# A fused cross-attention and feed-forward kernel: one weight factor split later, and one store of sums cut in three

## The chip, the cores and the metric

The kernel runs on one core of a Trainium2 chip. The metric is the device time of one execution in microseconds (us), the median of the runs. The core has a matrix engine (TensorE, PE in the profile, with its weight loads under PEld), three elementwise engines (VectorE or DVE, ScalarE or ACT, GpSimd or POOL) and SyncE (SP), whose queue issues nearly all of this kernel's transfers (DMAs). The engines run their own instruction streams in order and meet at semaphores.

## The reference, cut to what matters

```python
x = x + tanh(g_xattn) * attention(layernorm(x), ctx, ctx, Wq, Wk, Wv, Wo)   # 32 heads, 8 key/value heads
xt = layernorm(x).reshape(-1, 1024)                                        # 16 * 128 = 2048 tokens
x = x + tanh(g_ffn) * ((silu(xt @ W_gate.T) * (xt @ W_up.T)) @ W_down.T)   # hidden width 2752
```

Everything is float32. Each product is made from three matmuls of operands that are split in a high part, rounded to the matrix engine's format (`_h`), and the low rest (`_l`): high by high, high by low, low by high.

## The kernel before, in words

**Stages.** First the attention, in NG = 4 groups of four sequences (`body`). Then the feed-forward part in NS = 2 passes `s` over the tokens. Each pass has a gate/up phase and a down phase. Both use a scheme with seven products of half size instead of eight (Strassen-Winograd), so sums and differences of blocks are made ahead of the products.

**Gate/up.** For each of 21 blocks of hidden units (`quad`; the very first is `first_quad`) seven products are made. Product j takes the weight factor `w_h[j]`, `w_l[j]` and the token operand `xop_h[j]`, `xop_l[j]`. ACT makes the high part of a factor (`weight_hi`), DVE the low one (`weight_lo`). Factors 1, 2, 4 and 5 are sums of weight blocks that POOL makes into `fs`. In pass 0 the token operands are made around and inside the first quad: PE transposes a piece (`first_tokens(n)`, n = 0 to 27, four pieces for each operand) into one of two PSUM banks, ACT copies its high part (`first_tokens_hi`), DVE subtracts for its low part (`first_tokens_lo`). With only two banks, `first_tokens(n)` on PE waits until piece n-2 has its low part (`xp_lo`, n-1). In product 0 pieces 8 to 11 are transposed, one behind each of its four steps of the contraction, and so on. The fifth factor (j = 4) is copied by ACT once `xp_done` is 8 and `ts_ready` is 16, where 16 means that POOL has finished the last of the sums `t4`. This is needed because its place in memory was taken by other data until then. In the kernel before, this copy stands just ahead of `first_quad` on both ACT and DVE. On DVE there stand behind it five low parts (pieces 8 to 12), the halves of the attention's last addition (`add_half`), and its statistics, each between two low parts.

**Down.** The hidden values of two blocks are a pair; there are PAIRS_B = 11 pairs. POOL makes five sums of a pair in `hsum` (five matrices of 256 KB), and they are stored to DRAM in `hs`. A down phase has 77 steps, seven products (`m`) of eleven pairs (`q`). Step n has q = n mod 11. For each step SP loads two matrices of 256 KB into one of RAWS = 4 buffers `raw` (`load_down`: one from `hs`, one from `ws` or `wd`), ACT copies the high part (`bh`, one of three buffers, `down_hi`), DVE subtracts the low part (`bl`, `down_lo`), and PE runs four groups of three matmuls (in some steps of pass 0 with transposes for the next pass among them). `load_down(n)` waits until step n-4 has its low part. `down_hi(n)` waits until PE is through with step n-3. At a change of product (n = 11, 22, ...) DVE also adds the finished sums into `xo` (`add_down`).

**The place of the store.** SP issues in the order of the program. At the end of `gate_up` stand `load_down(7)`, `load_xo(C12)` (1 MB), `load_down(8)` and the store of the last pair's five sums (1280 KB in one DMA), which waits for POOL. Then `down` goes on with `load_down(9)`, `load_down(10)`, `load_down(11)`, `load_xo(C22)` (1 MB), `load_down(12)`. `load_down(11)` is the first step of the second product and waits until all eleven stores of sums of the pass have landed. POOL's `pair_sums` for pass 1 also waits for them, because its `ts` lies on `hsum`.

Of the kernel before, what the change touches and what calls it, by code (L numbers as in the profile page):

```python
# [99 lines left out]
def gated_cross_attention_ffn(nc, x, ctx_t, wc, wr, wf, wm, wd, g_xattn, g_ffn, x1d, hs, ws, out):  # L100

    with ExitStack() as ctx:
# [114 lines left out]
        def sem(name):  # L217
            return ctx.enter_context(nc.semaphore(name))
# [69 lines left out]
        h_ready = sem("h_ready")  # L288
        ha_out, hb_out, hs_out = sem("ha_out"), sem("hb_out"), sem("hs_out")
        hs_ready = sem("hs_ready")  # L290
        hb_zero = sem("hb_zero")
        dw_in = sem("dw_in")
        ws_ready, ws_out = sem("ws_ready"), sem("ws_out")
# [47 lines left out]
        def pairs(s, c, i):  # L341
            return i + (PAIRS_B * s + c // 2)
# [29 lines left out]
        def _(sp):  # L372
# [137 lines left out]
            def store_sums(s, c, i):  # L510
                sp.wait_ge(hs_ready, summed(s, c, i, H_SUMS))
                sp.sem_inc(passed, 1)
                sp.dma_start(of_pair(hs[s], i + c // 2)[0:H_SUMS].rearrange("m p n -> p m n"), hsum[:, :, :]).then_inc(hs_out, 16)

            def load_dw(q, i):
                if q == 0:
                    sp.wait_ge(xp_done, 28)
                else:
                    sp.wait_ge(ws_out, i * 32 + 32 * q)
                sp.sem_inc(passed, 1)  # L520
                src = wd[2 * q:2 * q + 2] if isinstance(i, int) else wd[bass.ds(i * 2 + 2 * q, 2)]
                sp.dma_start(dw[:, :, :], src.rearrange("t p n -> p t n")).then_inc(dw_in, 16)
# [9 lines left out]
            def load_down(s, n):  # L532
                m, q = n // PAIRS_B, n % PAIRS_B
                k = n % RAWS
                hx, wx, _ = DOWN[m]
                if n >= RAWS:
                    sp.wait_ge(b_lo, step(s, n - RAWS))
                elif n < 2:
                    sp.wait_ge(ws_out, 32 * PAIRS_B)
                elif n == 2:  # L540
                    sp.wait_ge(w_lo, splits(s, QUADS - 2, 0, PROD))
                else:
                    sp.wait_ge(w_lo, SPLITS * (s + 1))
                if m == 0:
                    sp.wait_ge(ha_out, 16 * (PAIRS_B * s + q + 1) + 1)
                elif q == 0:
                    sp.wait_ge(hs_out, 16 * PAIRS_B * (s + 1) + 1)
                    sp.wait_ge(hb_out, 16 * PAIRS_B * (s + 1) + 1)
                w = wd[2 * q, :, 0:HALF] if wx == W_B11 else wd[2 * q + 1, :, HALF:D] if wx == W_B22 else ws[q][wx]
                sp.dma_start(raw[k][:, 0, :], hs[s][q][hx]).then_inc(raw_in[k], 16)  # L550
                sp.dma_start(raw[k][:, 1, :], w).then_inc(raw_in[k], 16)

            def gate_up(s):
                load_fraw(s, 2, 0)
                if s == 0:
                    load_dw(0, 0)
                store_even(s, 0, 0)
                with sp.Fori(0, TRIPS) as i:
                    load_fraw(s, 3, i)
                    if s == 0:  # L560
                        store_ws(0, i)
                    store_odd(s, 1, i)
                    load_fraw(s, 4, i)
                    store_sums(s, 1, i)
                    if s == 0:
                        load_dw(1, i)
                    store_even(s, 2, i)
                load_fraw(s, QUADS, 0)
                if s == 0:
                    store_ws(PAIRS_B - 2, 0)  # L570
                    load_dw(PAIRS_B - 1, 0)
                load_down(s, 2)
                store_odd(s, QUADS - 2, 0)
                store_sums(s, QUADS - 2, 0)
                if s + 1 < NS:
                    load_xs(s + 1, 0)
                if s == 0:
                    store_ws(PAIRS_B - 1, 0)
                load_down(s, 0)
                load_down(s, 1)  # L580
                store_even(s, QUADS - 1, 0)
                for n in range(RAWS - 1, 7):
                    load_down(s, n)
                store_odd(s, QUADS, 0)
                load_down(s, 7)
                load_xo(s, C12)
                load_down(s, 8)
                store_sums(s, QUADS, 0)

            def place(c, s, dram, a, b):  # L590
                tiles = 8 * s + 4 * (c // 2)
# [23 lines left out]
            def down(s):  # L615
                more = s + 1 < NS
                for n in range(9, STEPS_B):
                    load_down(s, n)
                    if n == 11:
                        load_xo(s, C22)  # L620
                    elif more and n == 14:
                        load_xs(s + 1, 1)
                    elif n == 20:
                        load_xo(s, C11)
                    elif n == 32:
                        load_xo(s, C21)
                    elif more and n == 28:
                        load_xs(s + 1, 2)
                    elif more and n == 39:
                        load_xs(s + 1, 3)  # L630
                    elif n == 53:
                        store_out(s, C22, 3)
                    elif more and n == 61:
                        load_fraw(s + 1, 0, 0)
                    elif n == 64:
                        store_out(s, C21, 4)
                    elif n == 75:
                        store_out(s, C12, 5)
                if more:
                    load_fraw(s + 1, 1, 0)  # L640
                store_out(s, C11, ND - 1)
# [40 lines left out]
        def _(pool):  # L682
# [56 lines left out]
            def pair_sums(s, t):  # L739
                pool.wait_ge(xs_ready, 8 * s + 2 * t + 2)  # L740
                if t == 0:
                    pool.wait_ge(hs_out, 16 * PAIRS_B * s + 1)
                if t > 0:
                    pool.wait_ge(xp_done, 28 * s + 7 * t)
                b11, b21 = xs[t % 2][:, 0, 0:HALF], xs[t % 2][:, 0, HALF:D]
                b12, b22 = xs[t % 2][:, 1, 0:HALF], xs[t % 2][:, 1, HALF:D]
                made = 16 * s + 4 * t
                nc.gpsimd.tensor_tensor(ts[:, 0, :], b12, b11, ALU.subtract).then_inc(ts_ready, 1)
                pool.wait_ge(ts_ready, made + 1)
                nc.gpsimd.tensor_tensor(ts[:, 1, :], b22, ts[:, 0, :], ALU.subtract).then_inc(ts_ready, 1)  # L750
                nc.gpsimd.tensor_tensor(b12, b22, b12, ALU.subtract).then_inc(ts_ready, 1)
                pool.wait_ge(ts_ready, made + 2)
                nc.gpsimd.tensor_tensor(ts[:, 2, :], b21, ts[:, 1, :], ALU.subtract).then_inc(ts_ready, 1)
# [28 lines left out]

            def even_sum(s, c, i):
                pool.wait_ge(h_ready, twos(s, c, i, 2))
                pool.wait_ge(hs_out, 16 * pairs(s, c, i) + 1)
                nc.gpsimd.tensor_tensor(hsum[:, 4, :], hb[0][:, 1, :], hb[0][:, 0, :], ALU.subtract).then_inc(hs_ready, 1)

            def pair_of_h(s, c, i):
# [71 lines left out]
        def _(act):  # L860
# [178 lines left out]
            def first_quad():  # L1039
                act.wait_ge(o_done, NG * NB)  # L1040
                first_tokens_hi(range(8, 12))
                act.wait_ge(p_done, 1)
                act.wait_ge(x1_out3, 16)
                copy(x1c[:, :], ps[:, 0, :]).then_inc(x1c_ready, 1)
                first_tokens_hi(range(12, 18))
                weight_hi(0, 0, 0, 5)
                first_tokens_hi(range(18, 22))
                weight_hi(0, 0, 0, 6)
                first_tokens_hi(range(22, 24))
                act.wait_ge(x1_out, 16 * (BATCH - 1) + 1)  # L1050
                first_tokens_hi(range(24, 28))
                for j in range(2):
                    weight_hi(0, 1, 0, j)
                act.wait_ge(p_done, 4)
                nc.scalar.activation(hb[0][:, 0, :], ps[:, 0, :], ACT.Silu).then_inc(silu, 1)
                for j in range(2, 4):
                    weight_hi(0, 1, 0, j)
                act.wait_ge(comb, combs(0, 0, 0, 4))
                nc.scalar.activation(hb[0][:, 1, :], hb[0][:, 1, :], ACT.Silu).then_inc(silu, 1)
                for j in range(4, PROD):  # L1060
                    weight_hi(0, 1, 0, j)
# [66 lines left out]
            first_tokens_hi(range(4, 6))  # L1128
            first_tokens_hi(range(6, 8))
            weight_hi(0, 0, 0, 3)  # L1130
            weight_hi(0, 0, 0, 4)
            for s in range(NS):
                more = s + 1 < NS
                if s == 0:
# [22 lines left out]
        def _(dve):  # L1157
# [287 lines left out]
            def first_quad():  # L1445
                t = LAST_ORDER[3]
                first_tokens_lo(range(8, 13))
                dve.wait_ge(o_done, NG * NB)
                add_half(NG - 1, t, 0)
                first_tokens_lo(range(13, 14))  # L1450
# [95 lines left out]
            first_tokens_lo(range(6, 8))  # L1546
            weight_lo(0, 0, 0, 3)
            add_attention(NG - 1, LAST_ORDER[2], 2)
            weight_lo(0, 0, 0, 4)
            for s in range(NS):  # L1550
                more = s + 1 < NS
                if s == 0:
# [440 lines left out]
```

## Time and profile before

| what | value |
|---|---|
| median of 3 runs | 1900.26 us (1899.02 to 1903.03) |
| the profiled execution | 1900.98 us, of which the span of the trace is 1899.2 us |
| PE busy | 1887.4 us, 99% of the span |
| DVE, POOL, ACT busy | 1235.0, 866.5, 825.8 us (65%, 46%, 43%) |
| share of PE on the chain that ended last | 95% |
| granted clock of PE | 1.000 of full speed |
| DMA over the span | 298.78 MB, mean 157 GB/s |

The span is what the trace covers; the execution's own time is 1.8 us more. A busy share of 99% on PE means that only what lets PE wait can change the time much, or work taken from it. Idle time of the others costs nothing by itself.

### The profile page before, as it was taken

Reading aid. Unit: us, or ns where it says so; the run is one execution under the profiler, and the core shown is the slowest. Engines: PE = TensorE matmul, PEld = TensorE weight load, DVE = VectorE, ACT = ScalarE, POOL = GpSimd, SP = SyncE. Lnnn points to the kernel's source line nnn. Section 1 sums busy time; section 2 is a strip of 40 time slices with the busy share of each in tenths; the row PEclk is TensorE's granted clock in tenths of the full one; section 3 lists DMA queues with packets and bytes.
Section 4 is the critical chain, followed back from the end, with each engine's and each line's share of the span. In section 5 each row is a group of like instructions: output and inputs, shape, how many; then the busy total and the mean of one; then the engine's idle time right before and its main releaser. Section 6 shows DMA issues by size and latency. Waiting matters only on the chain.

```text
span 1899.2 us, 27364 instructions
## 1 busy us (share of the span) xinstructions
PE 1887.4 (99%) x9346; PEld 1555.7 (82%) x9346; DVE 1235.0 (65%) x1716; ACT 825.8 (43%) x1947; POOL 866.5 (46%) x632
## 2 busy tenths in 40 slices
PE   9999999999999999999999999999999999999999
PEld 7888888888888788888888788888888888888887
DVE  7877887787787855555554767665555555546565
ACT  5863773683584533333332444443333333333333
POOL 1430440251255598888887311116666766630000
PEclk9999999999999999999999999999999999999999
DMA  6335326326324345354536876752323232267675
GB/s 212 90 130 172 104 65 246 98 62 233 119 79 172 118 143 186 138 193 147 181 140 216 301 242 205 243 177 75 120 101 110 84 118 103 89 212 251 213 227 182
DMA packets 127196, 298.78 MB, mean 157 GB/s; under 512 B 12672, under 2 KB 24448, under 8 KB 121728
## 3 DMA queue, kind: packets, MB, share of 16 engines
q1 hardware_dynamic: 126960, 297.45, 46.3%
q8 instruction: 54, 0.88, 0.2%
q14 instruction: 38, 0.31, 0.1%
q10 hardware_dynamic: 144, 0.13, 0.0%
HBM read 221.25 MB, written 71.57 MB: 154 GB/s over the span
## 4 chain that ended last, share of the span: by engine, by line
PE 95%; DMA 2%; POOL 2%; DVE 1%; issue 0%; ACT 0%; SPq 0%; POOLq 0%; DVEq 0%; ACTq 0%
PE ps L1592 28%; PE ps L1594 28%; PE ps L1593 28%; PE ps L1642 3%; PE ps L1633 2%; PE ps L1653 2%; PE ps L1634 2%; PE ps L1804 1%; DMA raw<-ws 1%; PE ps L1690 1%; PE ps L1815 1%; DMA ws<-dw 1%; DMA kv_raw<-in_wc 0%; DMA dw<-in_wd 0%; DVE bl L1160 0%
## 5 line engine op out<-in xcount | busy, mean ns | idle before, releaser
L1592 PE MATMUL ps<-xop_h,w_h 128*128 128x512 f32 x1208 | 471.8, 391 | 0.0
L1594 PE MATMUL ps<-xop_h,w_l 128*128 128x512 f32 x1208 | 470.1, 389 | 0.0
L1593 PE MATMUL ps<-xop_l,w_h 128*128 128x512 f32 x1208 | 470.0, 389 | 0.0
L1160 DVE TENSOR_TENSOR bl<-raw,bh 128x1024 fp32r<-128x1024 f32 x154 | 199.5, 1304 | 143.1 <-ACT bh L862 142.8
L1594 PEld LDWEIGHTS ps<-xop_h,w_l 128*128 128x128 f32 x1208 | 226.7, 188 | 47.1
L1592 PEld LDWEIGHTS ps<-xop_h,w_h 128*128 128x128 f32 x1208 | 226.8, 188 | 46.6 <-DVE cc L1405 0.3
L1593 PEld LDWEIGHTS ps<-xop_l,w_h 128*128 128x128 f32 x1208 | 226.8, 188 | 46.4
L862 ACT ACTIVATE bh<-raw 128x1024 fp32r<-128x1024 f32 x154 | 163.0, 1061 | 225.9 <-PE ps L1594 195.9
L1160 DVE TENSOR_TENSOR w_l<-fraw,w_h 128x512 fp32r<-128x512 f32 x130 | 135.4, 1042 | 185.9 <-ACT w_h L862 185.9
L1592 PE MATMUL ps<-bh 128*128 128x512 f32 x616 | 243.0, 395 | 2.1 <-DVE bl L1160 2.0
L1594 PE MATMUL ps<-bh,bl 128*128 128x512 f32 x616 | 240.1, 390 | 0.0
L710 POOL TENSOR_TENSOR pb<-pb,rinv 128x512 f32<-128x512 f32 x128 | 154.8, 1211 | 186.7 <-DVE rinv L1216 186.7
L1593 PE MATMUL ps<-bl,bh 128*128 128x512 f32 x616 | 239.9, 390 | 0.0
L862 ACT ACTIVATE w_h<-fs 128x512 fp32r<-128x512 f32 x168 | 105.9, 632 | 287.9 <-PE ps L1594 272.1
L911 ACT ACTIVATE pb<-ps,nmx 128x128 f32<-128x128 f32 x512 | 181.3, 370 | 45.7 <-DVE nmx L1211 44.3
L1160 DVE TENSOR_TENSOR w_l<-fs,w_h 128x512 fp32r<-128x512 f32 x168 | 172.5, 1028 | 7.7 <-ACT w_h L862 7.7
L1592 PEld LDWEIGHTS ps<-bh 128*128 128x128 f32 x616 | 115.7, 188 | 27.1 <-DVE bl L1160 3.9
L1594 PEld LDWEIGHTS ps<-bh,bl 128*128 128x128 f32 x616 | 115.6, 188 | 24.5
L1593 PEld LDWEIGHTS ps<-bl,bh 128*128 128x128 f32 x616 | 115.8, 188 | 23.1
L778 POOL TENSOR_TENSOR hb<-hb,cc 128x512 f32<-128x512 f32 x42 | 54.2, 1291 | 169.2 <-ACT hb L1036 164.4
L911 ACT ACTIVATION_READ_ACCUMULATOR pb<-ps,nmx 128x1 f32 x512 | 106.3, 208 | 0.0
L1592 PE MATMUL ps<-wr_h,qo_h 128*128 128x512 f32 x256 | 104.6, 409 | 0.0
(158 smaller groups left out, 3408.6 us busy)
## 6 DMA issues: line engine op xcount, KB each, us to landing
fraw<-in_wf SPq DMA_DIRECT2D x42, 1024.0 KB, 5.2
raw<-hs SPq DMA_DIRECT2D x154, 256.0 KB, 3.1
hs<-hsum SPq DMA_DIRECT2D x22, 1280.0 KB, 5.8
raw<-ws SPq DMA_DIRECT2D x110, 256.0 KB, 4.0
wc_raw<-in_wc SPq DMA_DIRECT2D x44, 512.0 KB, 4.6
dw<-in_wd SPq DMA_DIRECT2D x11, 1024.0 KB, 7.7
hs<-hb SPq DMA_DIRECT2D x44, 256.0 KB, 2.1
raw<-in_wd SPq DMA_DIRECT2D x44, 256.0 KB, 4.1
```

The costliest lines, as they stand in the source:

```text
L710: nc.gpsimd.tensor_tensor(p, p, r, ALU.mult).then_inc(normed, 1)
L778: nc.gpsimd.tensor_tensor(h[:, 1, :], h[:, 1, :], cc[:, 1, :], ALU.mult).then_inc(h_ready, 1)
L862: return nc.scalar.activation(out, in_, ACT.Copy, scale=scale)
L911: ins = nc.scalar.activation(pb[:, n % 4, j * P:(j + 1) * P], ps[:, n % 3, j * P:(j + 1) * P], ACT.Exp, bias=nmx[:, n % 4, j:j + 1], accum ...
L1160: return nc.vector.tensor_tensor(out, whole, hi.bitcast(F32), ALU.subtract)
L1592: pe.matmul(out, w_hi_, m_h, start=first, stop=False, skip_group_check=goes_on)
L1593: pe.matmul(out, w_hi_, m_l, start=False, stop=False, skip_group_check=goes_on)
L1594: return pe.matmul(out, w_lo_, m_h, start=False, stop=last, skip_group_check=goes_on)
L1633: pe.matmul(ps[:, n % 3, cols], q[:, iq, toks], kb_h[:, b, cols], start=True, stop=False)
L1634: ins = pe.matmul(ps[:, n % 3, cols], q[:, iq, toks], kb_l[:, b, cols], start=False, stop=True)
L1642: ins = pe.transpose(ps[:, 3 + n % 2, j * P:(j + 1) * P], pb[:, n % 4, j * P:(j + 1) * P], ident[:, :])
L1653: ins = pe.matmul(ps[head, 5, m % 2 * 2 * P:(m % 2 + 1) * 2 * P], vc[:, b, k // 2 * P + HD * j:k // 2 * P + HD * j + HD], pt[:, m % 4, j, ...
```

## The change

Two parts. In the first quad, `weight_hi(0, 0, 0, 4)` moves on ACT behind the high parts of pieces 8 to 11, and `weight_lo(0, 0, 0, 4)` moves on DVE behind the low parts of pieces 8 to 12. In the down phases, the last pair's store of five sums (`store_sums(s, QUADS, 0)`) becomes three stores (`store_last_sums`) of two, two and one matrices, with a semaphore of their own, `hs_parts`. The first stands where the old store stood; the second behind `load_down(9)`, the third behind `load_down(10)`. `load_down` at a change of product and `pair_sums` wait for `hs_parts` too, and the counts of `hs_out` are one store less in each pass.

```diff
+            def store_last_sums(s, part):
+                own = slice(2 * part, min(2 * part + 2, H_SUMS))
+                if part == 0:
+                    sp.wait_ge(hs_ready, summed(s, QUADS, 0, H_SUMS))
+                sp.dma_start(hs[s][PAIRS_B - 1][own].rearrange("m p n -> p m n"), hsum[:, own, :]).then_inc(hs_parts, 16)
...
                 elif q == 0:
-                    sp.wait_ge(hs_out, 16 * PAIRS_B * (s + 1) + 1)
+                    sp.wait_ge(hs_out, 16 * (PAIRS_B - 1) * (s + 1) + 1)
+                    sp.wait_ge(hs_parts, 48 * (s + 1))
                     sp.wait_ge(hb_out, 16 * PAIRS_B * (s + 1) + 1)
...
                 load_down(s, 8)
-                store_sums(s, QUADS, 0)
+                store_last_sums(s, 0)
...
                 for n in range(9, STEPS_B):
                     load_down(s, n)
-                    if n == 11:
+                    if n < 11:
+                        store_last_sums(s, n - 8)
+                    elif n == 11:
                         load_xo(s, C22)
...
             def pair_sums(s, t):
                 pool.wait_ge(xs_ready, 8 * s + 2 * t + 2)
                 if t == 0:
-                    pool.wait_ge(hs_out, 16 * PAIRS_B * s + 1)
+                    pool.wait_ge(hs_parts, 48 * s)
...
             def even_sum(s, c, i):
-                pool.wait_ge(hs_out, 16 * pairs(s, c, i) + 1)
+                pool.wait_ge(hs_out, 16 * pairs(s, c, i) + (1 - 16 * s))
...
             def first_quad():                       # ACT
                 act.wait_ge(o_done, NG * NB)
                 first_tokens_hi(range(8, 12))
+                weight_hi(0, 0, 0, 4)
...
             weight_hi(0, 0, 0, 3)
-            weight_hi(0, 0, 0, 4)
...
             def first_quad():                       # DVE
                 first_tokens_lo(range(8, 13))
+                weight_lo(0, 0, 0, 4)
                 dve.wait_ge(o_done, NG * NB)
...
             add_attention(NG - 1, LAST_ORDER[2], 2)
-            weight_lo(0, 0, 0, 4)
```

## Rows read from the trace of the kernel before

**Rows 1.** Page, part 1: busy us, share of span, instructions.

```profile
PE 1887.4 (99%) x9346; PEld 1555.7 (82%) x9346; DVE 1235.0 (65%) x1716; ACT 825.8 (43%) x1947; POOL 866.5 (46%) x632
```

**Rows 2.** Waits of PE: line, releaser, us in total, times, longest.

```profile
PE ps L1592 <- DVE bl L1160: 2.0, 1, 2.0
PE ps L1804 <- DVE xop_l L1160: 1.8, 1, 1.8
```

**Rows 3.** Timeline, first quad, PE and PEld: start, duration, work, [idle before].

```profile
632.03 0.66 PE L1804 MATMUL ps<-ident,t 128*128 128x128 f32 x4 [1.83 <-DVE xop_l L1160]
...
637.61 0.47 PEld L1804 LDWEIGHTS ps<-ident,xa 128*128 128x128 f32 x4 [0.15 <-DVE xop_l L1160]
...
642.44 0.60 PE L1804 MATMUL ps<-ident,xb 128*128 128x128 f32 x4
```

**Rows 4.** Timeline, first quad, ACT.

```profile
630.02 0.63 ACT L862 ACTIVATE w_h<-fs 128x512 fp32r<-128x512 f32 x1 [7.05 <-PE ps L1804]
630.56 1.07 ACT L862 ACTIVATE xop_h<-ps 128x512 fp32r<-128x512 f32 x2
...
634.35 0.59 ACT L862 ACTIVATE x1c<-ps 128x512 f32<-128x512 f32 x1
```

**Rows 5.** Timeline, first quad, DVE.

```profile
629.33 0.64 DVE L1279 COPY mv<-mvx 128x2 f32<-128x2 f32 x1
630.69 0.69 DVE L1160 TENSOR_TENSOR w_l<-fs,w_h 128x512 fp32r<-128x512 f32 x1 [0.72 <-ACT w_h L862]
631.29 1.28 DVE L1160 TENSOR_TENSOR xop_l<-ps,xop_h 128x512 fp32r<-128x512 f32 x2
...
635.61 0.69 DVE L1160 TENSOR_TENSOR xop_l<-ps,xop_h 128x512 fp32r<-128x512 f32 x1 [0.43 <-ACT xop_h L862]
636.22 0.74 DVE L1260 SCALAR_TENSOR_TENSOR x<-ps,tg,x 128x512 f32<-128x512 f32 x1
```

**Rows 6.** Timeline, ahead of the first quad, POOL.

```profile
623.91 6.03 POOL L737 TENSOR_TENSOR t<-xa,t 128x512 f32<-128x512 f32 x4
```

**Rows 7.** Timeline, down phase of pass 0, SP: when a DMA is issued.

```profile
1065.08 0.39 SPq L513 DMA_DIRECT2D hs<-hsum  x1
...
1071.51 0.33 SPq L550 DMA_DIRECT2D raw<-hs  x1
```

**Rows 8.** DMA issues of two short windows: count, KB, us to landing.

```profile
hs<-hb SPq DMA_DIRECT2D x1, 256.0 KB, 2.0
...
raw<-ws SPq DMA_DIRECT2D x1, 256.0 KB, 3.0
```

**Rows 9.** Page, part 6: all loads of `ws`, median us to landing.

```profile
raw<-ws SPq DMA_DIRECT2D x110, 256.0 KB, 4.0
```

**Rows 10.** Windows of 2 us: busy of each engine, PE clock, DMA share, GB/s.

```profile
1070.00:1072.00 2.00, 2.00 (x11) 1.65 (x10) 0.24 (x1) 0.00 (x0) 0.41 (x1) 1.00 0.99 354
```

**Rows 11.** Timeline, down phase of pass 0, ACT: steps 9, 10, 11, 12.

```profile
1074.01 1.06 ACT L862 ACTIVATE bh<-raw 128x1024 fp32r<-128x1024 f32 x1 [5.02 <-DMA raw<-ws]
1075.28 1.06 ACT L862 ACTIVATE bh<-raw 128x1024 fp32r<-128x1024 f32 x1 [0.22 <-DMA raw<-ws]
1076.59 1.06 ACT L862 ACTIVATE bh<-raw 128x1024 fp32r<-128x1024 f32 x1 [0.25 <-DMA raw<-ws]
1080.98 1.07 ACT L862 ACTIVATE bh<-raw 128x1024 fp32r<-128x1024 f32 x1 [3.33 <-DMA raw<-ws]
```

**Rows 12.** Timeline, down phase of pass 0, PE: step 9 begins.

```profile
1076.61 0.50 PE L1592 MATMUL ps<-bh 128*128 128x512 f32 x1 [2.00 <-DVE bl L1160]
```

**Rows 13.** Timeline, down phase of pass 0, POOL.

```profile
1071.59 1.29 POOL L748 TENSOR_TENSOR ts<-xs 128x512 f32<-128x512 f32 x1 [6.62 <-DMA hs<-hsum]
```

**Rows 14.** Timeline, down phase of pass 1, ACT: steps 8, 10, 11, 12.

```profile
1702.84 1.06 ACT L862 ACTIVATE bh<-raw 128x1024 fp32r<-128x1024 f32 x1 [1.66 <-PE ps L1594]
...
1708.66 1.06 ACT L862 ACTIVATE bh<-raw 128x1024 fp32r<-128x1024 f32 x1 [0.26 <-DMA raw<-ws]
...
1711.00 1.06 ACT L862 ACTIVATE bh<-raw 128x1024 fp32r<-128x1024 f32 x1 [1.27 <-PE ps L1594]
...
1716.13 1.06 ACT L862 ACTIVATE bh<-raw 128x1024 fp32r<-128x1024 f32 x1 [4.07 <-DMA raw<-ws]
```

More of the change, by code:

```diff
@@ L290, in gated_cross_attention_ffn @@
         hs_ready = sem("hs_ready")
+        hs_parts = sem("hs_parts")
         hb_zero = sem("hb_zero")
```

## The prediction, made before the changed kernel was run

> **What bounds the kernel now.** I read the page's first part, then PE's waits, then the timeline around each place that the change touches. PE is busy 99% of the span at full granted clock, so the time is PE's work plus the few gaps in it [rows 1]. PE's own waits show which: among the whole kernel's there is one of 1.8 us for the low part of a token piece, in the first quad, and one of 2.0 us for a low part in a down phase [rows 2]. These two lie where the two parts of the change act. Together they are 3.8 us, 0.2% of the time, so that is about all that the change can gain; how much it can lose is open.
>
> **Part A, the fifth weight factor.** PE starts the transpose of piece 10 at 632.03 after 1.83 us idle; without a wait it would have begun at about 630.1 [rows 3]. It needs the low part of piece 8. That one starts on DVE at 631.29, and PE goes 0.74 us later [rows 3, 5]. Ahead of it in DVE's order stands the factor's low part (630.69), which had to wait for ACT's high part, and ACT made this at 630.02 [rows 4, 5]. The view names PE's transposes as the releaser of that copy, but those were over long before; the code also makes it wait for `ts_ready` 16, and POOL's last `t4` sum ends at 623.91 + 6.03 = 629.94 [rows 6]. So POOL's sums hold the factor, and the factor held pieces 8 and 9 on ACT, which were copied only at 630.56 [rows 4].
>
> After the change, piece 8 (transposed by about 628.4, an estimate from PE's round of 1.13 us) has its high part at about 629.0, well before DVE is free. DVE is busy with the attention's statistics until 629.33 + 0.64 = 629.97 [rows 5]; operations of this kind start back to back with an overlap of some 0.08 us (630.69 + 0.69 against 631.29 [rows 5]), so the low part starts at 629.9 in place of 631.29. PE then starts piece 10 at 629.9 + 0.74 = 630.64. **First gain: 1.39 us** of the 1.83; the rest of the gap is now DVE's own work.
>
> Where the factor goes it costs again. On ACT its copy (0.63 us) stands between piece 11's high part and the `x1c` copy of 0.59 us, which was at 634.35 [rows 4]. Before, ACT had 1.13 us per round for one piece and this copy, just enough; now there are two copies of about 0.50 us (starts overlap by 0.1) besides piece 11's own 0.50, so piece 12 comes 1.5 us behind piece 11 instead of 1.13: 0.39 us late. Its low part, at 635.61 before [rows 5], comes 1.39 - 0.39 = 1.0 us earlier. From there DVE is the tight engine: the addition follows at 636.22 without idle time [rows 5], and for the next rounds PE's loads wait on low parts, first by 0.15 us at 637.61; at 642.44 PE is free of that [rows 3]. The factor's low part now stands at the head of this stretch and takes 0.60 us of it (the start-to-start spacing of 630.69 and 631.29). So all that follows on DVE is earlier by 1.0 - 0.6 = 0.4 us, and PE behind it. **Part A: -0.4 us.** Bounds: -1.4 if PE had enough slack on pieces 13 to 17 to ride out the 0.6 (rows 3 speak against it), and 0 if the two insertions together cost the whole gain. Nobody else is hurt: product 4 reads the factor only some 10 us later, and SP has nothing in this part. Past the first quad PE has no wait until the down phase, so the 0.4 is kept.
>
> **Part B, pass 0.** One step of PE is 2.72 us: the high parts of steps 8 and 11 in pass 1, both released by PE, are three steps apart, (1711.00 - 1702.84) / 3 [rows 14]. Step 9 is late because its load is: ACT waits 5.02 us for it, until 1074.01; PE starts the step at 1076.61, 2.60 us after ACT, and had been idle for 2.00 us [rows 11, 12]. Call a step's deadline the start of its high part at which PE would just not wait. For step 9 it is 1072.0, then 1074.7, 1077.4 and 1080.2 for steps 10, 11, 12. Against these the landings (ACT starts within 0.1 us of them) were 1074.0, 1075.3, 1076.6, 1081.0 [rows 11]. The queue is full in this stretch, a DMA share of 0.99 at 354 GB/s with PE at full clock [rows 10]: everything lands in about the order and at the rate of its bytes.
>
> The store of 1280 KB is issued at 1065.08 just ahead of loads 9 and 10, and its landing at 1071.5 releases load 11 and POOL [rows 7, 13]. Cut in three, 768 KB less stand ahead of load 9, and 256 KB less ahead of load 10. At 0.35 MB per us with a discount for the slower stores (0.3) that is 2.5 and 0.8 us: landings at 1071.5 and 1074.5, both inside the deadlines. **The 2.0 us wait at step 9 goes.** What is late next is load 11. It waits for all the parts, and the third stands behind load 10: it can't land before the bytes ahead of it, the same bytes as before, have gone, at about 1075.2, when load 10 landed before. So load 11 is issued at 1075.2, not 1071.51 [rows 7], and by then the queue has run dry, because SP holds `load_xo` and load 12 behind the waiting load 11. Into an idle queue the second matrix of a step, issued 0.4 us after the first, takes 3.0 us [rows 8]: load 11 lands at 1078.7, 1.25 us past its deadline. Load 12 stands behind 1 MB for `xo`; the three loads took 1080.98 - 1075.28 = 5.7 us of full queue [rows 11], and now start flowing 1.9 us later (3.0 less the 0.7 us that 256 KB take and the 0.4 between the two issues): landing at about 1082.9, 2.7 us past the old deadline. So PE waits 2.7 us in all (at steps 11 and 12) instead of 2.0, plus up to 0.4 for DVE, whose additions of step 10 stand ahead of step 12's low part: I take **+0.9 us**, between +0.3 and +1.5.
>
> The Trainium skill bears on this point. Its page "DMA: Bandwidth & Descriptors", section "Queues, rings and completion order", says that a DMA's semaphore increment lands only after every earlier write of the same DMA engine. By that, the third part cannot be reported ahead of load 10, which is the sum's assumption; the trace agrees as far as it goes, since the store and the load behind it landed within 0.3 us of each other. The same page's section on the anatomy of one DMA gives a fit of 2.0 us plus bytes over 436 GB/s for one on its own, 2.6 us for 256 KB; taken alone it would have the third part land early, which is the first rival below.
>
> POOL's `pair_sums` moves with the last landing from 1071.59 to about 1075.3 [rows 13]. Its transposes belong to step 14, some 15 us on, and its four operations take about 6, so that cover holds. It ran beside the low parts of steps 9 to 11 before and runs beside that of step 11 now; I cost this at nothing more than the 0.4 above. The two further DMA issues cost SP 0.39 us each [rows 7], while it waits anyway.
>
> **Part B, pass 1.** No wait of PE there, though steps 10 and 12 wait for their loads, at 1708.66 and 1716.13 [rows 2, 14]. Step 12's natural time is 1711.00 + 2.72 = 1713.7; the deadline lies 2 x 2.72 + 0.2 - 2.60 = 3.1 us behind it (0.2 as in pass 0, where PE's modelled end reaches over), at 1716.8, so it had 0.7 us to spare. The third part now lands at about 1708.6 with load 10, load 11 is issued then and lands at 1712.0, inside its deadline of 1714.1. But `xo` and load 12 again start flowing 1.9 us later: 1718.0, and PE waits **+1.2 us** at step 12. Bounds: 0, if the queue catches up (this stretch took 7.5 us from 1708.66 to 1716.13 where pass 0 took 5.7), and +1.6.
>
> **The sum.** -0.4 + 0.9 + 1.2 = +1.7 us on the profiled execution's 1900.98, so 1902.7. That execution was 0.7 above the median of 1900.26; on the median it is **1902.0 us**. About 0.2% (3.8 us) is what a measurement of this kernel can tell from no change, so this counts as the same.
>
> **Rivals.** *The third part lands early.* If stores pass the loads ahead of them, 256 KB landed in 2.0 us [rows 8]; issued at about 1071, it would release load 11 at about 1073, the queue would never run dry, and step 9's 2.0 us would be gained whole: -0.4 - 2.0 = -2.4, 1897.9 us. For it: 2.0 us is what such a store took. Against it: in a full queue the big store landed with the load behind it. *The bubble is shorter.* If the queue refills in half the time (the first bytes 1 us after the issue), load 12 is 1 us less late in both passes: 1.7 - 2.0 = -0.3, 1900.0. *The bubble is longer, and the kernel slower.* The median load of `ws` takes 4.0 us over the whole kernel, not 3.0 [rows 9]. If the restarted queue gives such a landing, and the 1 MB for `xo` is as slow, loads 11 and 12 are 1.1 us later in both passes: 1.7 + 2.2 = +3.9, and with 0.5 of DVE beside POOL +4.4, 1904.7. It decides from a restart of about 3 us; rows 8 against rows 9 is the question. *The change does nothing there*: if the DMA engines reordered the parts anyway, only part A is left, 1899.9, inside the second case.
>
> **How the numbers follow.** Forecast (1900.8 to 1903.5): 0.50. Early landing: 0.16. Shorter bubble or no effect: 0.24. Longer bubble: 0.10, about half of it over 0.2%. The runs before spread by 4 us, so each case is blurred by about 1 us. The range takes in the early landing and most of the long bubble: 1897.7 to 1904.2. Faster by over 0.2% needs more than the two waits hold: 0.02. Slower by over 0.2%: 0.06. Same: 0.92.
>
> **What the profile after would show.** Part A: piece 10's transpose with some 0.5 us idle, more waits of 0.2 to 0.7 us on low parts about pieces 14 and 15, and the first quad's end 0.4 us earlier. Part B, pass 0: ACT's wait for step 9 over by 1072, no PE wait there; load 11 issued at about 1075 instead of 1071.5; then PE waits of about 1.2 us at step 11 and 1.5 us at step 12; a dip in the DMA share between 1075 and 1077. Pass 1: one wait of about 1.2 us at step 12. The prediction is wrong if load 11 is issued before 1074, if PE shows no wait in pass 1, or if the piece-10 gap goes whole without new ones behind it.

## The result, and the profile after

The changed kernel takes 1904.28 us (median of 13 runs, 1901.80 to 1908.00) against 1901.05 us for the kernel before. The ratio is 1.0019, 95% interval [1.0011, 1.0027]: 2.1 to 5.1 us slower. The forecast of 1902.0 us had the sign and most of the mechanism, but its change of +1.7 us is half of the measured one (+3.2 by the medians, +3.6 by the ratio), and the range ended at 1904.2. It also started from a median of three runs, 1900.26; thirteen give 1901.05. The profiled execution, 1902.64 us with a span of 1900.8, is one of the quickest of the thirteen and hides a part of the loss, as will be seen.

**Part A, the first quad.** The timeline of PE in the changed kernel (start, duration, work, [idle before]). `L1815` is the transpose of a token piece:

```profile
631.24 0.66 PE L1815 MATMUL ps<-ident,t 128*128 128x128 f32 x4 [0.44 <-DVE xop_l L1171]
...
637.79 0.66 PE L1815 MATMUL ps<-ident,xa 128*128 128x128 f32 x4 [0.50 <-DVE xop_l L1171]
```

The gap of 1.83 us [rows 3] is 0.44 now, and a second one of 0.50 stands where the factor's low part meets the attention's additions on DVE. DVE in the same place:

```profile
635.18 0.69 DVE L1171 TENSOR_TENSOR xop_l<-ps,xop_h 128x512 fp32r<-128x512 f32 x1 [0.80 <-ACT xop_h L873]
635.79 0.68 DVE L1171 TENSOR_TENSOR w_l<-fs,w_h 128x512 fp32r<-128x512 f32 x1
636.39 0.74 DVE L1271 SCALAR_TENSOR_TENSOR x<-ps,tg,x 128x512 f32<-128x512 f32 x1
```

The piece (`xop_l`) comes late by ACT (0.80 us of idle DVE), then the factor (`w_l`) and the addition follow without a gap. In [rows 5] the addition followed the piece directly.

**Part B, pass 0.** SP, ACT, POOL, DVE and PE in the down phase of pass 0, each from its timeline:

```profile
1070.19 0.50 SPq L521 DMA_DIRECT2D hs<-hsum  x1
1074.63 0.33 SPq L559 DMA_DIRECT2D raw<-hs  x1
...
1071.31 1.06 ACT L873 ACTIVATE bh<-raw 128x1024 fp32r<-128x1024 f32 x1 [2.38 <-DMA raw<-ws]
1073.88 1.06 ACT L873 ACTIVATE bh<-raw 128x1024 fp32r<-128x1024 f32 x1 [1.51 <-DMA raw<-ws]
1078.13 1.06 ACT L873 ACTIVATE bh<-raw 128x1024 fp32r<-128x1024 f32 x1 [3.19 <-DMA raw<-ws]
1083.99 1.06 ACT L873 ACTIVATE bh<-raw 128x1024 fp32r<-128x1024 f32 x1 [4.79 <-DMA raw<-ws]
...
1074.62 1.29 POOL L759 TENSOR_TENSOR ts<-xs 128x512 f32<-128x512 f32 x1 [9.13 <-DMA hs<-hsum]
...
1082.59 2.07 DVE L1508 SCALAR_TENSOR_TENSOR xo<-ps,tg,xo 128x512 f32<-128x512 f32 x3 [1.44 <-DMA xo<-x1d]
...
1083.39 0.50 PE L1603 MATMUL ps<-bh 128*128 128x512 f32 x1 [1.21 <-DVE xo L1508]
1084.71 0.50 PE L1603 MATMUL ps<-bh 128*128 128x512 f32 x1 [0.34 <-DVE xo L1508]
1086.36 0.50 PE L1603 MATMUL ps<-bh 128*128 128x512 f32 x1 [0.69 <-DVE bl L1171]
```

Steps 9 and 10 are in time (1071.31 and 1073.88 against 1074.01 and 1075.28 in [rows 11]), and PE's wait at step 9 [rows 12] is gone. But the third part, issued at 1070.19, lands only at 1074.6 (POOL starts with it), and with it load 11 is released, 3.1 us later than in [rows 7]. Load 12 lands at 1084.0 instead of 1081.0. PE waits three times, 2.24 us together. Two of the three end in an addition on DVE that waited for the 1 MB of `xo`: this load, too, stands behind load 11. The queue ran dry meanwhile, as the windows of 2 us show (the last three columns are PE's clock, the DMA share and GB/s):

```profile
1070.00:1072.00 2.00, 2.00 (x11) 1.65 (x10) 0.18 (x1) 0.69 (x1) 0.00 (x0) 1.00 1.05 386
1072.00:1074.00 2.00, 2.00 (x10) 1.67 (x9) 1.23 (x1) 0.49 (x2) 0.00 (x0) 1.00 0.59 227
1074.00:1076.00 2.00, 2.00 (x10) 1.67 (x9) 1.02 (x1) 0.94 (x1) 1.30 (x2) 1.00 0.09 20
1076.00:1078.00 2.00, 2.00 (x10) 1.65 (x10) 1.00 (x1) 0.00 (x0) 2.00 (x1) 1.00 0.82 303
```

In pass 1 this execution has no wait of PE at all; load 12 of pass 1 came at 1717.91, just inside its deadline.

One more wait of PE, 0.49 us at about 1058, stands ahead of the store, where part B has no instruction. Ten of the seventeen traces have it, with 0.2 to 0.9 us, before's not. The waits given below for the down phases leave it out.

### The profile page after: what moved, and what is told of

Read it like the earlier page. It is cut to its first block, busy times and chain, and to the rows that moved or that the text cites. A ratio compares the mean times of both kernels' runs of the same rounds, so it can differ in the third digit from the quotient of the medians.

```text
span 1900.8 us, 27378 instructions
## 1 busy us (share of the span) xinstructions
PE 1888.7 (99%) x9346; PEld 1555.3 (82%) x9346; DVE 1235.3 (65%) x1716; ACT 825.9 (43%) x1947; POOL 867.6 (46%) x632
## 4 chain that ended last, share of the span: by engine, by line
PE 93%; DMA 2%; DVE 2%; POOL 1%; issue 1%; ACT 0%; SPq 0%; POOLq 0%; DVEq 0%; ACTq 0%
PE ps L1603 28%; PE ps L1605 28%; PE ps L1604 28%; PE ps L1653 3%; PE ps L1644 2%; PE ps L1664 2%; PE ps L1645 2%; DMA raw<-ws 1%; PE ps L1701 1%; PE ps L1826 1%; DVE bl L1171 1%; DMA ws<-dw 1%; PE ps L1815 0%; DMA kv_raw<-in_wc 0%; DMA dw<-in_wd 0%
```

## The experiments

All are compared with the kernel before on the same chip. "Under 1.000" counts the executions whose mean granted clock over the whole span was 0.999 or less.

| run | what | median | before | ratio [95%] | under 1.000 |
|---|---|---|---|---|---|
| e1_a | part A alone | 1900.40 | 1902.48 | 0.9992 [0.9983, 1.0001] | 4 of 11 |
| e2_b | part B alone | 1904.74 | 1902.48 | 1.0014 [1.0005, 1.0023] | 10 of 11 |
| e3_late3 | changed, wait at load 21 | 1898.54 | 1902.48 | 0.9983 [0.9974, 0.9992] | 0 of 11 |
| e4_late1 | one store, wait at load 21 | 1900.71 | 1902.48 | 0.9997 [0.9988, 1.0006] | 3 of 11 |
| e5_run | three parts in one run | 1899.55 | 1900.40 | 0.9993 [0.9984, 1.0002] | 0 of 11 |
| e6_xo | xo ahead of load 11 | 1901.40 | 1900.40 | 1.0003 [0.9994, 1.0012] | 1 of 11 |
| e8_gap3 | e3 and a wait of 0.75 us | 1899.51 | 1900.40 | 0.9992 [0.9983, 1.0001] | 0 of 11 |
| e9_gap4 | e3 and a wait of 2.01 us | 1901.63 | 1900.40 | 1.0006 [0.9997, 1.0015] | 5 of 11 |
| e9b_gap5 | e3 and a wait of 3.27 us | 1904.14 | 1901.12 | 1.0012 [1.0003, 1.0021] | 10 of 11 |
| e10_gate0 | early wait in pass 0 only | 1901.21 | 1901.12 | 1.0000 [0.9991, 1.0009] | 3 of 11 |
| e11_gate1 | early wait in pass 1 only | 1899.85 | 1901.12 | 0.9997 [0.9988, 1.0006] | 4 of 11 |
| e12_late3_noa | e3 without part A | 1899.70 | 1901.12 | 0.9990 [0.9981, 0.9999] | 4 of 11 |
| e13_safe | e3 with its memory guarded | 1898.88 | 1901.53 | 0.9985 [0.9976, 0.9994] | 0 of 11 |
| e14_after | the changed kernel again | 1906.41 | 1901.53 | 1.0021 [1.0012, 1.0030] | 8 of 11 |
| e15_safe_run | e13 with the parts in one run | 1899.37 | 1901.53 | 0.9987 [0.9978, 0.9996] | 0 of 11 |

The kernel before itself was under 1.000 in 22 of 33, 11 of 33, 14 of 33 and 14 of 27 executions, on the four chips in the order of the table. Differences between rows with different "before" are taken from the ratios. Six of the seventeen traces are of executions under 1.000 (`e1_a`, `e2_b`, `e9_gap4`, `e9b_gap5`, `e10_gate0`, `e14_after`). In each of them the 2 us windows show one stretch at half clock at a wait of PE, some 3.4 us long in four of them and some 6.8 us in `e9b_gap5` and `e14_after`. The eleven others show none ahead of the last 1.3 us of the kernel.

**Which part: e1_a, e2_b.** e1_a is the diff of `weight_hi` and `weight_lo` alone, e2_b all the rest.

> Part A alone on the kernel before; the store of sums is one DMA as before. My theory (part B holds the loss, part A brings 0.4 us): 0.4 us less than before, and the gap of 2.0 us at step 9 of pass 0 stays as it was. Rival (the gaps that part A makes in the first quad cost more than they bring, or lower the granted clock): at least 1.5 us more than before, with PE waits behind piece 13 that add up to more than 1.8 us.

> Part B alone. My theory: the whole loss of the changed kernel is here, so 3.2 + 0.4 = 3.6 us more than before in the median; load 11 is issued at about 1075, and PE waits some 2.5 to 4 us in pass 0 between steps 11 and 13. Rival (part A is to blame): within 1 us of before.

The loss is part B's: +2.7 us (1.0 to 4.4). Part A is at -1.5 us (-3.2 to +0.2), which takes in both nothing and the forecast -0.4; its rival, a loss of 1.5 us or more, is out. In e1_a PE's two waits in the first quad are 0.41 and 0.51 us, and the wait at step 9 is there, 1.80 us, with a half-clock stretch behind it. In e2_b PE has these:

```profile
1084.42 0.79 PE L1603 MATMUL ps<-bh 128*128 128x512 f32 x1 [2.46 <-DVE xo L1507]
...
1723.40 0.50 PE L1603 MATMUL ps<-bh 128*128 128x512 f32 x1 [1.63 <-DVE bl L1171]
```

So pass 1 has a wait too in this execution, which the changed kernel's profile did not show. And the first matmul behind the wait took 0.79 us instead of 0.50. The windows say why; the clock, in the third column from the end, was at half for a part of them:

```profile
1082.00:1084.00 2.00, 0.00 (x0) 0.00 (x0) 0.39 (x1) 0.00 (x0) 0.00 (x0) 1.00 1.04 385
1084.00:1086.00 2.00, 1.58 (x4) 1.10 (x5) 1.68 (x3) 0.98 (x1) 0.00 (x0) 0.52 1.05 412
1086.00:1088.00 2.00, 2.00 (x6) 1.09 (x6) 1.83 (x2) 1.49 (x3) 0.00 (x0) 0.62 1.02 406
1088.00:1090.00 2.00, 2.00 (x10) 1.68 (x9) 2.00 (x4) 0.70 (x1) 0.00 (x0) 1.00 0.88 321
```

**The gate: e3_late3, e4_late1.** Only the last pair's step of the second product (n = 21) reads what the parts store. The edit in e3_late3:

```diff
                 elif q == 0:
-                    sp.wait_ge(hs_parts, 48 * (s + 1))
...
+                if n == 2 * PAIRS_B - 1:
+                    sp.wait_ge(hs_parts, 48 * (s + 1))
```

> The changed kernel with one edit: the wait for the three parts moves from load 11 to load 21, the first load that reads the last pair's sums. My theory (the cost comes from load 11 waiting for the third part while the queue runs dry): load 11 is issued by 1072, no dip of the DMA share at 1075, PE waits at steps 9 to 13 of pass 0 under 0.5 us, and the time 2.0 + 0.4 = 2.4 us under before. Rival (three stores among the loads are themselves the cost, through slower landings): the time stays at that of the changed kernel, 3 us over before, though load 11 is early.

> The kernel before, one store of 1280 KB at its old place, but the wait for it moved to load 21. My theory: load 9 still stands behind 1280 KB, so PE's 2.0 us at step 9 stays; load 11 comes 2 to 4 us earlier, which helps nobody: within 0.5 us of before. Rival (what counts is load 11's issue alone, and the split is useless): as fast as the kernel with three parts and the late wait.

The late wait turns +3.6 into -3.2 us, more than the 2.4 us under before that I had expected; the rival, that three stores are themselves the cost, falls. PE has no wait in its down phases but one of 0.29 us at about 1058. e4_late1 (one store, the same late wait, no part A) keeps its 1.89 us at step 9 and is not told from before: the late wait alone does not take that wait away.

One thing has to be said of both: the `xo` of C22 lies on the first two matrices of `hsum`, and the early wait also kept its load from overwriting them. These two, and e6, e8, e9, e9b, e10, e11 and e12, issue that load without this guard in at least one pass. They show where time goes; none is a version to keep.

**Bytes or number of stores: e5_run, e6_xo.** e5_run issues the three parts in a loop where the first stood; e6_xo loads `xo` at n = 10 instead of 11.

> The changed kernel, but the three parts are issued directly one behind the other, where the first stood, and loads 9 and 10 come behind them; the wait stays at load 11. Theory (what counts is how many bytes stand ahead of load 9 and when load 11 is released, not the number of stores): it behaves as part A alone, within 1 us of it, PE waits 1.8 to 2 us at step 9 of pass 0 and not at steps 11 to 13. Rival (three stores cost by themselves): 2 us or more over part A alone.

> The changed kernel with the 1 MB load for xo moved ahead of load 11, so that the queue has bytes while load 11 waits. Theory (the queue running dry is the cost): the dip of the DMA share at 1075 is filled, DVE no longer waits for xo, but load 11 now stands behind up to 1 MB: it lands no earlier, so PE waits about 1 to 1.5 us at step 11 and nothing at steps 10 and 12 in pass 0; 1 to 3 us under the changed kernel. Rival (the late issue of load 11 alone is the cost, whatever else the queue does): the same time as the changed kernel, within 0.7 us.

e5_run is at -1.3 us, like part A alone (-1.5), so three stores cost nothing by their number. Its waits miss the expectation: 0.26 us at step 9 and 0.70 at step 12, not 1.8 to 2. Load 9 is hardly earlier than behind one store of the same 1280 KB (ACT starts at 1071.71 in e5_run, at 1072.03 in e1_a). The larger part is DVE: step 9's low part takes 1.38 us in e5_run and 2.31 us in e1_a, where POOL's `pair_sums` run beside it. So POOL, which the landed store releases, holds step 9 too. In e1_a and e4_late1 load 9 landed 2.0 and 1.6 us sooner than before's 1074.01 (PE itself was 0.9 and 0.7 us ahead of before's), and PE waited 1.8 and 1.9 us all the same, with low parts of 2.3 us. In the changed kernel POOL starts only at 1074.62, and the low part, started at 1072.40, takes 1.23 us. How much of the gain at step 9 is POOL's and how much is the load's was not tried apart. The forecast put it all down to the load. e6_xo is 3 us under the changed kernel by its ratio, and PE waits 0.96, 0.29 and 0.16 us, the first at step 11, as expected. The rival of an unchanged time falls: with bytes in the queue the early wait costs less.

**Where: e10_gate0, e11_gate1.** The early wait is kept in one pass only.

> The changed kernel with the early wait (at load 11) kept in pass 0 only; in pass 1 the wait stands at load 21. Theory (my sum gave pass 0 a wait of 2.7 us or more against none with the late wait in both): PE waits 2 to 3.5 us in pass 0, none in pass 1; 3 to 4 us over the kernel with the late wait in both passes, since part of the executions also lose clock. Rival (pass 1 holds the larger part): under 1.5 us over it.

> The mirror: the early wait kept in pass 1 only. Theory: PE waits 0 to 1.6 us at step 12 of pass 1 and not in pass 0; 0.5 to 2 us over the kernel with the late wait in both passes. Rival (pass 1 costs nothing, as the profile of the changed kernel suggests, which has no wait there): within 0.4 us of it.

Against the late wait in both passes (0.9983) these are +3.2 us for pass 0 and +2.7 us for pass 1, across chips and with intervals of 1.7 us on either side. The sum, -3.2 + 3.2 + 2.7 = +2.7, agrees with the measured +3.6 within the error. e10_gate0 is as expected, with PE waits of 2.20 and 0.35 us in pass 0. e11_gate1 is above its expectation, and its executions fall apart: seven at 1899.25 to 1900.20 with clock 1.000, four at 1902.93 to 1903.63 with 0.999. Its profile is of the first kind, with a PE wait of 0.16 us in pass 1.

**The price of a wait: e8_gap3, e9_gap4, e9b_gap5.** From e3_late3, with extra subtractions on DVE ahead of one step's low part, in a quiet stretch (the edit of e9_gap4; the others have 3 and 5):

```diff
             def down_lo(s, n):
...
+                if s == 1 and n == 40:
+                    for j in range(4):
+                        minus(bl[n % RING][:, :, :], raw[n % RAWS][:, :, :], bh[n % RING][:, :, :]).then_inc(pad, 1)
+                        dve.wait_ge(pad, j + 1)
```

> The kernel with the late wait, which has no long PE wait in its down phases, plus three extra subtractions on DVE ahead of step 40's low part in pass 1 (a quiet stretch without transposes or additions). With a slack of 3.1 us and some 1.25 us for each this makes one PE wait of about 0.8 us. Theory (a wait of PE costs its own length, and a long one in some executions also a few us at half clock): +0.8 us, no execution with a mean clock under 1.000. Rival (the lower clock has nothing to do with the length of the wait): clocks under 1.000 as often as in the kernel before.

> The same with four extra subtractions: one PE wait of about 2.1 us, as long as the one that the kernel before has at step 9. Theory: +2.1 us in the executions that stay at full clock, and in some third of them another 1.5 to 2 us, because matmuls run at the 1.2 GHz level for some 3 to 4 us behind the wait; mean clock 0.999 or less there. Rival: only +2.1 us, a narrow spread as in the kernel without the wait.

> Five extra subtractions ahead of step 40's low part in pass 1: one PE wait of about 3.4 us. Theory: +3.4 us and the half-clock stretch in at least half of the executions, more often than behind the wait of four subtractions. Rival: as often, or never.

The waits of PE behind the extra work, one line from each, in this order:

```profile
1794.07 0.50 PE L1609 MATMUL ps<-bh 128*128 128x512 f32 x1 [0.75 <-DVE bl L1173]
```

```profile
1794.09 0.50 PE L1609 MATMUL ps<-bh 128*128 128x512 f32 x1 [2.01 <-DVE bl L1173]
...
1795.44 0.63 PE L1611 MATMUL ps<-bh,bl 128*128 128x512 f32 x1
1795.87 0.63 PE L1609 MATMUL ps<-bh 128*128 128x512 f32 x1
1796.30 0.63 PE L1610 MATMUL ps<-bl,bh 128*128 128x512 f32 x1
```

```profile
1797.46 0.80 PE L1609 MATMUL ps<-bh 128*128 128x512 f32 x1 [3.27 <-DVE bl L1173]
```

None of eleven executions is under full clock with 0.75 us, five with 2.01 us, ten with 3.27 us. In the second one the matmuls start 0.43 us apart from 1795.4 on, against 0.23 before: the 1.2 GHz level instead of 2.4. On the same chip the median of e9_gap4 is 2.1 us over e8_gap3, for 1.26 us more of wait. Its five executions under 1.000 have a median of 1902.64, its six others 1900.8. The rivals of all three fall. In the traces the matmuls that before's has from 1790 to 1800 take 1.1, 3.9 and 6.1 us longer: the wait of 2.01 us cost nearly twice its length.

**Part A once more: e12_late3_noa.**

> The kernel with the late wait, without part A. Theory (part A is worth 0.4 us and independent of the rest): 0.4 us over the kernel with both. Rival (the 1.8 us gap in the first quad also costs clock in some executions, so part A is worth more): 1 us or more over it, with some executions under a mean clock of 1.000.

0.9990 against 0.9983 is 1.3 us, with intervals that overlap. The count goes the same way: with the 1.9 us gap in the first quad and no wait in the down phases, 4 of 11 executions are under 1.000 (1900.26 to 1900.73, against 1898.5 for the median at full clock); with part A none, on another chip. This is the rival's picture, but it is not shown: of the four traces that have the gap of 1.8 to 1.9 us in the first quad (before, e2_b, e4_late1, e12_late3_noa) none has a half-clock stretch behind it.

**A version that beats both: e13_safe, and e14_after, e15_safe_run beside it.** e13_safe is e3_late3 with the missing guard:

```diff
-hsum[:, own, :]).then_inc(hs_parts, 16)
+hsum[:, own, :]).then_inc(hs_first if part == 0 else hs_parts, 16)
...
             def load_xo(s, c):
+                if c == C22:
+                    sp.wait_ge(hs_first, 16 * (s + 1))
```

with `hs_parts` counted to 32 in a pass, and `pair_sums` waiting for both.

> The kernel with the late wait, made whole: the first part (the two matrices that share their memory with xo of C22) has its own semaphore, and the load of that xo waits for it; the other two parts are waited for at load 21. Theory (the first part has landed by 1071, when the xo load comes up, so this wait is free): within 0.4 us of the late wait without it, 2 to 3 us under before, no execution under a mean clock of 1.000, PE waits under 0.7 us in the down phases. Rival (the wait for the first part empties the queue again): 1 us or more slower than that, with a DMA dip near 1071.

> The changed kernel once more, on the same chip as the other two. Theory: 3 us over before, 5 to 6 us over the safe late wait; of its executions, half or more with a mean clock under 1.000, and these 2 us or more over the rest; the profile has PE waits of 2 to 4 us in pass 0 that end in a low part or an addition to xo of DVE, and in pass 1 from 0 to 2 us. Rival (the waits alone make the difference): the executions at full clock are as slow as those below it.

> The safe late wait, with the three parts issued directly one behind the other ahead of load 9. Theory (the order of the bytes counts): load 9 lands later by what stands ahead of it, PE waits 0.3 to 2 us at step 9 in pass 0; 0.5 to 1.5 us over the interleaved version. Rival (the interleaving is worth nothing): within 0.3 us of it.

The guard costs nothing that can be told from noise: 0.9985 against 0.9983. PE waits 0.46 us in pass 0 (1.0 with the wait at 1058, over the 0.7 expected). e13_safe is 2.9 us (1.1 to 4.6) faster than before and 7.5 us faster than the changed kernel on the same chip (1898.88 against 1906.41; 6.9 by the ratios), more than the 5 to 6 us expected, with a spread of 2.7 us against 6.8. Its queue stays full in the windows in which it drained above:

```profile
1072.00:1074.00 2.00, 2.00 (x10) 1.66 (x9) 1.19 (x1) 0.46 (x1) 0.00 (x0) 1.00 1.06 375
1074.00:1076.00 2.00, 2.00 (x11) 1.65 (x10) 1.37 (x1) 0.60 (x1) 1.61 (x2) 1.00 0.94 337
```

e15_safe_run has a wait of 0.87 us at step 9 that e13_safe does not have, but is only 0.5 us slower in the median: what the interleaving itself is worth can't be told from noise. The changed kernel's second profile shows both things that the first one hid, a wait in pass 1 and a long stretch at half clock:

```profile
1083.02 0.50 PE L1603 MATMUL ps<-bh 128*128 128x512 f32 x1 [1.59 <-DVE xo L1508]
1084.34 0.50 PE L1603 MATMUL ps<-bh 128*128 128x512 f32 x1 [0.35 <-DVE xo L1508]
1085.98 0.79 PE L1603 MATMUL ps<-bh 128*128 128x512 f32 x1 [0.67 <-DVE bl L1171]
...
1724.35 0.50 PE L1603 MATMUL ps<-bh 128*128 128x512 f32 x1 [1.20 <-DVE bl L1171]
```

```profile
1084.00:1086.00 2.00, 0.99 (x4) 0.51 (x4) 1.52 (x3) 1.72 (x2) 0.00 (x0) 0.80 1.03 411
1086.00:1088.00 2.00, 2.00 (x5) 1.61 (x6) 2.00 (x3) 1.06 (x1) 0.00 (x0) 0.50 1.02 384
1088.00:1090.00 2.00, 2.00 (x7) 1.52 (x6) 2.00 (x3) 0.00 (x0) 0.00 (x0) 0.50 0.96 329
1090.00:1092.00 2.00, 2.00 (x6) 1.61 (x5) 0.99 (x2) 0.50 (x1) 0.00 (x0) 0.50 0.94 295
```

Here the three waits of pass 0 total 2.61 us, and the matmuls behind them run at half clock for some 6 us, at a cost of about 2.6 us (thirteen matmuls, 0.20 us more each). The half-clock stretch costs as much as the waits themselves. The rival of e14_after falls: its three executions at full clock have a median of 1903.76, its eight others 1906.5.

## Why the prediction was wrong, step by step

- **Part A: right, as far as the traces go.** The first gap fell by 1.39 us as worked out (1.83 to 0.44), and DVE's stretch took it back to 0.4: the changed kernel's profile runs 0.62 us behind before's ahead of the first quad (the addition at 626.84 against 626.22) and 0.18 behind it at the end (642.20 against 642.02), so -0.44. All thirteen traces with part A are 0.41 to 0.46 us quicker through the first quad than before's, matmul by matmul, and the three without it are within 0.03. Whether it is worth more in time (-1.5 by e1_a, with an interval that takes in -0.4) through the clock, as e12 hints, stays open.
- **Part B, the mechanism: right in the main.** Step 9's wait goes (by the load, and by POOL's later start, which the forecast did not count); load 11 is issued at 1074.63 (forecast 1075.2); the queue empties; load 12 is late. e3 and e13 show that the early wait is the cause. I forecast load 11's landing at 1078.7 and it was 1078.1; load 12's at 1082.9, and it was 1084.0, 1083.6, 1085.0 and 1085.0 in the four traces with the early wait in pass 0 (changed, e14_after, e2_b, e10_gate0).
- **Part B, pass 0, the waits: right in size, wrong in name.** 2.7 us were forecast. The same four profiles have 2.24, 2.61, 2.46 and 2.55 us. The forecast had 1.2 us at step 11 for its load and 1.5 at step 12; in the changed kernel step 11 begins without a named wait and step 12 has 0.69. I counted DVE's additions as an order of work worth up to 0.4 us; in fact they waited for the `xo` load behind load 11, and PE's waits for them were 1.55, 1.94, 2.46 and 2.55 us.
- **Part B, pass 1, the waits: right in place, high on average.** 1.2 us were forecast; four profiles show 0 (changed), 1.20 (e14_after), 1.63 (e2_b) and 0.16 (e11_gate1). It varies with when load 12 lands, and this is why the one profile beside the result looked like a confirmation of +1.7 (its time was 1.66 us over before's profile) while the median said more.
- **The step that failed: the sum priced each wait at its own length at full clock, with no term for the clock.** I read a granted clock of 1.00 in the one profile of before [rows 10] and took it as given. It was luck: the kernel before is under 1.000 in 61 of 126 executions, and so are 14 of the 24 of the changed kernel. For the changed kernel beside it on one chip, the three executions at full clock have a median of 1903.76 against 1900.83 for before's at full clock, +2.9 us; its eight others are at 1906.5 (+2.7 over its own full-clock ones), before's fourteen others at 1902.4 (+1.6). Weighted by how often they come, the lower clock costs the changed kernel 8/11 x 2.7 = 2.0 us and before 14/27 x 1.6 = 0.8: a difference of 1.2 us, which with the 2.9 gives 4.1; the ratio gives 4.0. The traces show it too: from 1060 to 1100 of pass 0 the changed kernel's first trace, at full clock, is 1.1 us slower than before's, matmul by matmul (forecast +0.9), and e14_after's, with the half-clock stretch, 4.1. A sum of waits is a lower bound here.
- **A second term was too small: a wait costs more than its idle time.** The profile draws a 128x512 matmul 0.39 us long, but at full clock they start 0.23 us apart, and the first one behind a wait has its successor 0.34 us behind it. So a wait costs 0.16 + 0.11 = 0.27 us beyond the idle time named, and a short one is not named at all. PE in the changed kernel:

```profile
1080.14 0.39 PE L1605 MATMUL ps<-bh,bl 128*128 128x512 f32 x1
1080.53 0.50 PE L1603 MATMUL ps<-bh 128*128 128x512 f32 x1
1080.87 0.40 PE L1604 MATMUL ps<-bl,bh 128*128 128x512 f32 x1
...
1081.80 0.39 PE L1605 MATMUL ps<-bh,bl 128*128 128x512 f32 x1
1083.39 0.50 PE L1603 MATMUL ps<-bh 128*128 128x512 f32 x1 [1.21 <-DVE xo L1508]
1083.73 0.40 PE L1604 MATMUL ps<-bl,bh 128*128 128x512 f32 x1
```

Before has one wait here, 2.00 + 0.27 = 2.3 us. The changed kernel has three and the short one at 1080.53, 2.24 + 4 x 0.27 = 3.3 us. The idle times alone would give +0.2 us; with this term they give the 1.1 by which the traces differ, but for 0.1.

- **What stays open.** The executions at full clock differ by 2.9 us beside each other; in the result's own thirteen runs the seven at full clock have a median of 1903.97. With the mean waits of the traces (2.5 us in pass 0, 0.75 in pass 1), 0.27 us more for each wait and part A's -0.4, I estimate +1.9. A hidden stretch at half clock is not the likely rest: one of 3.4 us brings the mean to 0.999, and the traces at 1.000 show none. Only three executions stand on one side of the 2.9, and none of them was traced. The runs don't settle it.
- **The rivals.** The early landing did not occur: the third part took 4.3 us, not the 2.0 of [rows 8], and landed at 1074.6, after load 10 at 1073.8. The Trainium skill, "DMA: Bandwidth & Descriptors", section "Queues, rings and completion order", has a DMA's semaphore raised only after all earlier writes of the same DMA engine; the trace agrees. The fit of 2.6 us that the prediction takes from the same page of the Trainium skill stands there in "Anatomy of one DMA — SWDGE (gpsimd) path", for DMAs that GpSimd issues; this store is issued by SP, behind others, and took 4.3 us. The longer bubble was half there: the second transfer of load 11 took 3.0 us from issue to landing, as forecast, but load 12 behind the 1 MB came 0.7 to 2.1 us later than forecast, where that rival said 1.1. Its 1904.7 lies near the measured 1904.28 all the same by luck: the waits did not grow with it (2.24 to 2.61 us against the 2.7 forecast), and the clock, which no rival named, made part of the time.

## What to carry to other kernels

A transfer that is cut in parts and spread among loads lands with its last part; look at every wait that counts the whole, and ask what stands in the queue behind the waiting instruction, before the cut. If the wait guards two things (here memory that the first part frees, and data that only a later step reads), give each its own semaphore at its own place: that was worth 7.5 us here. And where TensorE is busy 99% of the time, one wait of 2 us costs more than 2 us (3.9 us in e9_gap4's trace), so read the granted clock and the spread of the runs, not one profile.

## What the runs showed of the hardware

A wait of TensorE of 0.75 us, in a stretch that was otherwise full, left the clock at 2.4 GHz in all eleven executions; one of 2.01 us was followed by a lower mean clock in five of eleven, and one of 3.27 us in ten of eleven. Where it fell, 128x512 matmuls started 0.43 us apart instead of 0.23, for about 3.4 us behind the wait of 2.01 us, in e9_gap4's trace, and some 6 us behind the waits of 2.61 us in the changed kernel's second one. At full clock too a wait cost about 0.27 us more than the idle time that the profile names.

A subtraction of 128x1024 on DVE took 1.2 us alone and 2.3 us beside POOL's subtractions (step 9's low part, 1.23 us in the changed kernel, 2.31 in e1_a). And a store of 256 KB behind loads in a full queue landed 4.3 us after its issue, against 2.0 us in a nearly empty one [rows 8].
